# Identity products on TensorE at stage openings and in gaps, and four scale buffers in grouped attention

## What is computed

```python
x = x + tanh(g_xattn[0]) * L0_xattn(layernorm(x), ctx)        # latent attention
x = x + tanh(g_ffn[0])   * L0_ffn(layernorm(x))               # int8 weights
x = x + tanh(g_xattn[1]) * L1_xattn(layernorm(x), ctx)        # plain attention
x = x + tanh(g_ffn[1])   * L1_ffn(layernorm(x))               # memory slots, top 8 of 256
x = x + tanh(g_xattn[2]) * L2_xattn(layernorm(x), ctx, ctx)   # grouped attention, 32 heads of 32
x = x + tanh(g_ffn[2])   * L2_ffn(layernorm(x))               # 4-bit codes, Hadamard turn
x = x + tanh(g_xattn[3]) * L3_xattn(ctx, layernorm(x))        # 16 nearest points, gathered
x = x + tanh(g_ffn[3])   * L3_ffn(layernorm(x))               # top 2 of 8 low-rank experts

def quantize_weight(w):                                       # L2_ffn, both weights
    scale = maximum(max(abs(w), axis=-1) / 7, 1e-8)
    return clip(round(w / scale), -8, 7) * scale
```

## Time and profile before

| what | value |
| --- | --- |
| median of three runs | 2946.02 us (2936.29 to 2954.54) |
| the profiled execution, its own time | 2947.02 us |
| its span in the trace | 2945.2 us |
| mean granted clock of PE | 0.947 |
| PE busy / DVE busy | 90% / 64% |

### The profile page before, as it was taken

One profiled execution on the slowest core, in us unless ns is written; L12 is line 12 of the kernel. 1 busy time (PEld: TensorE's weight loads), 2 busy tenths in 40 slices (PEclk: granted clock), 3 DMA queues, 4 the chain that ended last, 5 costly groups with the idle time before them and its releaser, 6 DMA issues. The chain is left out here.

```text
span 2945.2 us, 50211 instructions
## 1 busy us (share of the span) xinstructions
PE 2654.0 (90%) x18888; PEld 1853.1 (63%) x18892; DVE 1884.9 (64%) x3362; ACT 1070.3 (36%) x2474; POOL 566.4 (19%) x610
## 2 busy tenths in 40 slices
PE   7999999999999489997878899998878999878888
PEld 4665765766656178885645555555557878656664
DVE  5546446456452776666557667677647988966774
ACT  3433433433333333331324444443435555312221
POOL 0110101101101210000024334444412333300000
PEclk9999999999999789998889899998889999988998
DMA  7110101101100655553464456554160001434421
GB/s 263 49 36 14 36 13 49 36 13 49 35 7 1 247 167 151 150 147 121 168 227 139 127 151 172 164 172 143 44 217 16 23 23 45 127 130 172 173 86 38
DMA packets 153764, 304.69 MB, mean 103 GB/s; under 512 B 83936, under 2 KB 107136, under 8 KB 144056
## 3 DMA queue, kind: packets, MB, share of 16 engines
q1 hardware_dynamic: 127064, 229.90, 24.1%
q0 software_dynamic: 19376, 57.15, 6.6%
q10 hardware_dynamic: 7120, 15.01, 1.8%
HBM read 246.39 MB, written 43.04 MB: 98 GB/s over the span
## 5 line engine op out<-in xcount | busy, mean ns | idle before, releaser
L1588 DVE TENSOR_REDUCE latent_nmax<-bank 112x1 f32<-112x487 f32 x128 | 85.2, 666 | 245.8 <-PE bank L1453 238.1
L2260 PE MATMUL bank<-ffn_qT,gather_whole 128*128 128x128 bf16 x3584 | 209.3, 221 | 16.7 <-ACT ffn_us L2383 5.9
L2002 POOL TENSOR_SCALAR grouped_probs<-grouped_probs,grouped_rsum 112x375 f32<-112x375 f32 x256 | 159.6, 642 | 311.8 <-DVE grouped_rsum L2055 311.5
L2260 PEld LDWEIGHTS bank<-ffn_qT,gather_whole 128*128 128x128 fp8e4 x3584 | 205.5, 99 | 21.5 <-issue 20.3
L1376 POOL TENSOR_SCALAR latent_probs<-latent_probs,latent_rsum 112x487 f32<-112x487 f32 x128 | 88.1, 688 | 636.9 <-DVE latent_rsum L1593 636.9
L1949 ACT ACTIVATE grouped_probs<-bank,grouped_nmax 112x375 f32<-112x375 f32 x256 | 143.3, 572 | 117.0 <-DVE grouped_nmax L2051 117.0
L2443 POOL TENSOR_TENSOR ffn_h<-ffn_sl,ffn_us 128x512 f32<-128x512 f32 x56 | 127.8, 2282 | 278.0 <-ACTq L2386 278.0
L1413 PEld LDWEIGHTS bank<-latent_hT,latent_wq 128*128 128x128 f32 x1536 | 175.3, 192 | 7.3 <-issue 7.1
L2051 DVE TENSOR_REDUCE grouped_nmax<-bank 112x1 f32<-112x375 f32 x256 | 122.4, 541 | 83.1 <-PE bank L1860 80.2
L1413 PE MATMUL bank<-latent_hT,latent_wq 128*128 128x112 f32 x1536 | 175.1, 275 | 0.0
L1391 PE MATMUL bank<-latent_wv,latent_hT 128*125 128x384 f32 (+1 forms) x512 | 168.8, 491 | 0.0
(11 more groups left out here) (419 smaller groups left out, 5424.4 us busy)
## 6 DMA issues: line engine op xcount, KB each, us to landing
grouped_raw<-L_weights SPq DMA_DIRECT2D x24, 2048.0 KB, 8.7
points_spread<-numbers SPq DMA_DIRECT2D x16, 912.0 KB
codes<-grouped_flip SPq DMA_DIRECT2D x24, 512.0 KB, 2.6
latent_hT<-ctxT SPq DMA_DIRECT2D x8, 1500.0 KB
plain_ctxT<-ctxT POOLq DMA_DIRECT2D x8, 1500.0 KB
plain_ctx<-ctx POOLq DMA_DIRECT2D x8, 1500.0 KB
grouped_ctx<-ctxT SPq DMA_DIRECT2D x8, 1500.0 KB, 6.6
gather_whole<-numbers SPq DMA_DIRECT2D x12, 912.0 KB
```

Source lines behind the costliest of these rows:

```text
L2002: pool.tensor_scalar(pr[:, g % 2, j, :], pr[:, g % 2, j, :], rsum[:, g % 2, j:j + 1], 1.0, ALU.mult, ALU.mult)\
L2260: mm = pe.matmul(ahead.tile(t)[:, i * P:(i + 1) * P], wgu[:, u0 + f // 4, c:c + 2 * P - 1:2], qT[:, k, :], start=(k == 0), stop=(k == KC - 1))
```

## The change

`kept_busy(pe, C, tile, n)` multiplies the identity by the identity n times into a bank that nobody reads before it is written anew. It stands at the opening of plain_attention (14 times), memory_ffn (16) and hadamard_ffn (22, after a wait for z), before the transposes of memory_ffn's last group (9), before `turned(g, 0)` of the first three quads of grouped_attention (8 each) and before each look of the first 16 rounds of gather_experts (3 each), 133 in all. Where it stands before a wait for data, the wait for the free bank was moved ahead of it. In grouped_attention `scale` gets four slots, `measured(u)` waits for the stores of unit u - 4, and `rounding(u, 0)` waits until unit u - 2 is turned, which frees its slot of `code`. `Norm` packs its three small tiles into one.

```diff
--- before.py
+++ after.py
@@ -265,9 +265,9 @@
 
     def __init__(self, s, n, rows=Q, name="ln"):
         self.stats = s.sb(f"{name}_stats", [rows, n, 2, 6])
-        self.mv = s.sb(f"{name}_mv", [rows, n, 2])
-        roots = s.sb(f"{name}_roots", [rows, 2, n, 1])
-        self.std, self.rstd = roots[:, 0], roots[:, 1]
+        rest = s.sb(f"{name}_mv", [rows, 4 * n])
+        self.mv = rest[:, 0:2 * n].rearrange("p (n c) -> p n c", c=2)
+        self.std, self.rstd = (rest[:, (2 + i) * n:(3 + i) * n].rearrange("p (n c) -> p n c", c=1) for i in range(2))
         self.var_ready = s.sem(f"{name}_var_ready")
         self.std_ready = s.sem(f"{name}_std_ready")
 
@@ -572,6 +572,12 @@
                 pool.tensor_tensor(x[:, b, :], x[:, b, :], bi[:], ALU.add).then_inc(bias_added, 1)
 
 
+def kept_busy(pe, C, tile, n):
+
+    for _ in range(n):
+        pe.matmul(tile[:, 0:P], C.ident[:], C.ident[:], start=True, stop=True)
+
+
 def turn_rows(pe, C, turns, src, name, s, p, n=2, rows=Q):
 
     for h in range(n):
@@ -662,6 +668,7 @@
         @block.tensor
         def _(pe):
             pe.wait_ge(wq_loaded, 16)
+            kept_busy(pe, C, banks.tile[7], 14)
             for s in range(2):
                 pe.wait_ge(z_ready, s + 1)
                 turn_rows(pe, C, first, z[:, s], "zT", s, 0)
@@ -1008,8 +1015,10 @@
             def weights(p):
                 for s in range(size(p)):
                     t = ("wT", p, s)
+                    pe.wait_ge(turns.free(t), turns.count(t, 0))
+                    if p == GROUPS - 1:
+                        kept_busy(pe, C, turns.tile(t), 9)
                     pe.wait_ge(w_ready, p * 2 + (s + 1))
-                    pe.wait_ge(turns.free(t), turns.count(t, 0))
                     for c in range(2):
                         mm = pe.transpose(turns.tile(t)[:, c * P:(c + 1) * P], w[:, s, c * P:(c + 1) * P], C.ident[0:P, 0:P])
                     mm.then_inc(turns.full(t), 1)
@@ -1034,6 +1043,7 @@
                         pe.matmul(turns.tile(t)[0:P, :], vT[:, s * P:(s + 1) * P], wvuT[:, h * 512:(h + 1) * 512], start=True,
                                   stop=True).then_inc(turns.full(t), 1)
 
+            kept_busy(pe, C, banks.tile[7], 16)
             turned(0)
             query(0)
             hidden(0, 0)
@@ -1653,7 +1663,7 @@
         raw, flip = s_.sb("raw", [P, 2, 4 * D]), s_.sb("flip", [P, 16, P], BF16)
         spare_code = spare["wu1T"][:].rearrange("p k n -> p (k n)")
         code, pairs = (spare_code.bitcast(dt).rearrange("p (s n) -> p s n", s=2) for dt in (FP8, BF16))
-        scale, rscale, part = s_.sb("scale", [P, 2, 4]), s_.sb("rscale", [P, 2, 4]), s_.sb("part", [P, 4])
+        scale, rscale, part = s_.sb("scale", [P, 4, 4]), s_.sb("rscale", [P, 2, 4]), s_.sb("part", [P, 4])
         CH = 114
         idx, point, hi, turned_numbers = (raw[:, 0, i * D:(i + 1) * D] for i in range(4))
         idx, turned_numbers = idx.bitcast(U32), turned_numbers.bitcast(BF16)
@@ -1754,7 +1764,7 @@
                 sp.dma_start_transpose(flip[:], pairs[:, u % 2, :]).then_inc(code_turned, 16)
                 sp.wait_ge(code_turned, 16 * (u + 1))
                 sp.dma_start(codes[wall_row(u)], flip[:].rearrange("p t r -> p (t r)").bitcast(U32)).then_inc(code_stored[u % 2], 16)
-                sp.dma_start(scales[wall_row(u)], scale[:, u % 2, :]).then_inc(code_stored[u % 2], 16)
+                sp.dma_start(scales[wall_row(u)], scale[:, u % 4, :]).then_inc(code_stored[u % 2], 16)
 
             def normal(n):
                 if n >= 1:
@@ -1862,9 +1872,11 @@
 
             def turned(g, k):
                 t = ("pT", g, k)
+                pe.wait_ge(turns.free(t), turns.count(t, 0))
                 if k == 0:
+                    if g < 3:
+                        kept_busy(pe, C, turns.tile(t), 8)
                     pe.wait_ge(probs_ready, 4 * g + 4)
-                pe.wait_ge(turns.free(t), turns.count(t, 0))
                 for j in range(4):
                     mm = pe.transpose(turns.tile(t)[0:CT, j * Q:(j + 1) * Q], pr[:, g % 2, j, k * CT:(k + 1) * CT], C.ident[0:Q, 0:Q])
                 mm.then_inc(turns.full(t), 1)
@@ -2012,16 +2024,16 @@
             def measured(u):
                 slot = u % 2
                 dve.wait_ge(raw_loaded[slot], u // 2 * 16 + 16)
-                if u >= 2:
-                    dve.wait_ge(code_stored[slot], u // 2 * 32)
+                if u >= 4:
+                    dve.wait_ge(code_stored[slot], (u // 2 - 1) * 32)
                 for i in range(4):
-                    to = scale[:, slot, i:i + 1] if u % 3 < 2 else part[:, i:i + 1]
+                    to = scale[:, u % 4, i:i + 1] if u % 3 < 2 else part[:, i:i + 1]
                     dve.tensor_reduce(to, raw[:, slot, i * D:(i + 1) * D], AX, ALU.max, apply_absolute_value=True)
                 dve.drain()
 
             def scaled(u):
                 slot, m = u % 2, 4 if u % 3 < 2 else 1
-                sc, rs = scale[:, slot, 0:m], rscale[:, slot, 0:m]
+                sc, rs = scale[:, u % 4, 0:m], rscale[:, slot, 0:m]
                 if m == 1:
                     dve.tensor_reduce(sc, part[:], AX, ALU.max)
                     dve.drain()
@@ -2033,6 +2045,8 @@
 
             def rounding(u, i):
                 dve.wait_ge(raw_scaled, 4 * u + i + 1)
+                if i == 0 and u >= 2:
+                    dve.wait_ge(code_turned, 16 * (u - 1))
                 dve.tensor_scalar(code[:, u % 2, i * D:(i + 1) * D], raw[:, u % 2, i * D:(i + 1) * D], MAGIC, 7.0, ALU.subtract, ALU.min, saturate=False)
                 if i == 3:
                     dve.drain().then_inc(raw_free, 1)
@@ -2261,6 +2275,8 @@
                                                start=(k == 0), stop=(k == KC - 1))
                         mm.then_inc(ahead.full(t), 1)
 
+            pe.wait_ge(z_loaded, 16)
+            kept_busy(pe, C, banks.tile[7], 22)
             entered(0, 0)
             gate_and_up(0, lambda j: pe.wait_ge(gu_loaded[j // 2], 32) if j % 2 == 0 else None)
             pe.wait_ge(wd_loaded, 16 * 3)
@@ -2736,8 +2752,10 @@
                 t = ("look", u)
                 if k == 0 and b > 0:
                     pe.wait_ge(table_ready, b)
+                pe.wait_ge(turns.free(t), turns.count(t, 0))
+                if u < K:
+                    kept_busy(pe, C, turns.tile(t), 3)
                 pe.wait_ge(onehot_ready, u + 1)
-                pe.wait_ge(turns.free(t), turns.count(t, 0))
                 for j in range(KC):
                     for n in range(3):
                         mm = pe.matmul(turns.tile(t)[:, j * RA:(j + 1) * RA], onehot[0:ROWS, u % 3, j * P:(j + 1) * P],
```

## The result

The changed kernel took 2921.78 us (median of 5 runs, 2918.79 to 2928.72) against 2942.27 for the kernel before in the same set (5 runs): a ratio of 0.9939, interval 0.9912 to 0.9965. The medians lie 20.5 us apart; the ratio of the runs says 18. Forecast were 2923 us and 22.9 us saved. By the bound of the prediction this is "within 1%", clear of noise and on the side forecast.

A forecast was written before the change was run, and what follows sets the result against it. PE, busy 90% of the span, was taken as the bound. Terms 21.3 + 2.3 + 0.2 + 1.0 + 1.6 - 3.5 = 22.9 us off 2947.0 gave 2924.1, 2923 us against the median; range 2904 to 2939.

The forecast's parts named there:

- opening 5.9 (6.0 forecast): Grouped attention ahead of batch 0: DVE begins unit 2 earlier, held by its load and no longer by stores; 6.0 us saved.
- 8.2 and 1.7 of clock forecast: Grouped attention, batches 2 to 5: PE's closed gaps save 8.2 us; full clock for batch 2's L1816 records saves 1.7.
- Rival 3: Grouped attention: DVE waits as long for raw to land, so 21.2 us of removed waits go; 2944 us, chance 0.06.
- the rounding's wait: Grouped attention: rounding's new wait for unit u - 2's turning is free, as its stores landed before rounding begins; 0 us.
- memory_ffn, 0.2 + 1.0 forecast: memory_ffn: a clock rise among the opening's products gains 0.2 us; nine hidden products before the last group gain 1.0.
- hadamard_ffn, 1.6 forecast: hadamard_ffn's opening: 22 products raise the clock, end 0.6 us late and gain 2.2 us of turning and L2260; 1.6 net.
- gather, 3.5 lost forecast: gather_experts, first batch: PE sets the pace, 4.3 us lost, 1.0 more at low clock, 1.8 taken up; 3.5 lost.
- The 24 products of grouped attention, 2.1 lost forecast: Products before the first three quads' turning: 0.2 us lost at the first, hidden at the second, 1.9 lost at the third.
- rival 1: Clock stays up through grouped attention's batches 0 and 1, with 1.0 us more in memory_ffn; 2917 us, chance 0.17.
- The clock across transposes: Plain attention's opening: by the skill's page the clock would fall during sixteen transposes, losing 2.3 us; the trace spoke against it.
- rival 2: The clock does not answer to the products: openings' 5.6 us go and 7.1 of delays are paid; 2936 us, chance 0.13.
- rival 4: All that follows shifts against the clock's regulation, causing drops of 1.7 us each; 2950 us with 16 drops, chance 0.04.

The follow-up runs named there:

- run 1: The changed kernel without any of the 133 products, the new waits kept: 2917.35 us, ratio 0.9916 to the kernel before.
- Run 8: The changed kernel, but a unit's first rounding waits for both stores of unit u - 2 instead of its turning: 2924.14 us, ratio 0.9942 to the kernel before.
- run 6: The changed kernel without gather's and grouped attention's products, with memory_ffn's gaps filled (6 before first L1004; 15, 2, 7 in last group): 2912.35 us, ratio 0.9899.
- run 5: The changed kernel without the products of gather, grouped attention and memory_ffn's last group; waits and three openings stay: 2919.96 us, ratio 0.9919.
- run 3: The changed kernel without the three products before each look of gather's first 16 rounds: 2920.13 us, ratio 0.9926 to the kernel before.
- run 9: The changed kernel's waits with products in memory_ffn alone (16 at its opening, then 6, 15, 2 and 7): 2919.49 us, ratio 0.9920 to the kernel before.
- run 2: The changed kernel with all 133 products, but measuring waits for unit u - 2 as before the change: 2948.5 us, ratio 1.0024 to the kernel before.
- run 11: The changed kernel with six products instead of three before each of gather's first 16 looks: 30.68 us from first look to first L2731, 22.53 with three.

## Why the prediction was right, and which terms were not

**The sum held, and in grouped attention by the mechanism named.** That the whole sum came so near is in part luck: memory_ffn, hadamard_ffn and the gather gave 4.8 us less than forecast, grouped and plain attention 3.2 more. Of the 23.4 us that the prediction gave to waits and clock in grouped attention, run 1 shows 23.9 without any product: opening 5.9 (6.0 forecast), 3.3 in batch 0 (from the first L1869 to the second L1883), 3.1 more up to the L1883 behind batch 1's gap (7.0 forecast for the two, 6.4 measured), and 11.6 behind that (8.2 and 1.7 of clock forecast, 9.9). The part mis-sized is the last. 0.7 of it is one more L1816 group that the shorter gap of batch 1 left at a higher clock (3.79 us before, 3.08 in run 1). The four gaps that closed in batches 2 to 5 gave 4.9, 2.7, 2.4 and 1.0 us from one L1883 to the next, 11.0 in all. Of that 1.7 is the clock, as forecast, and 9.3 stand against 8.2: the prediction added up idle times, but a gap of 2.47 us, once closed, brought the next start 2.73 us forward. Measuring started at 1515.07 with the change and at 1515.96 in run 1, against "about 1515.8". Rival 3, waits replaced by equal ones, has fallen (4.5 us of 27.5 came back, the part counted on). Run 8 shows that the rounding's wait is free, and the stronger wait too.

**The products, term by term.** All kernels run the same code in plain attention but for the 14 products: with them nine traces show 316.3 to 322.8 us (mean 320.4), without them four show 322.0 to 323.2 (mean 322.5). That is 2.2 us, against 2.3 forecast, but single traces of one kind lie up to 6.5 us apart. At the opening itself it is more: the first L697 stands 57.0 to 57.6 us behind the first L276 instead of 60.5 to 60.7. Some 3.4 are gained, and over a microsecond of it goes again to later falls of the clock.

- **memory_ffn, 0.2 + 1.0 forecast, 0 measured.** The failed step is the prediction's premise that what is saved at a place moves the end by as much. From the end of plain attention to L950 14.07 us replace 15.35: 1.3 gained (0.2 forecast). From there to the last L1004 the changed kernel takes 86.42 us instead of 84.82, as the stretch at 1.2 GHz after the 1.58 us gap lasted 13.7 us instead of 10.2. The last group gave 0.25 instead of 1.0, as the nine products left the gaps behind them open (run 6).
- **hadamard_ffn, 1.6 forecast, 0 measured.** Eleven of the thirteen traces have 444.9 to 445.4 us for the stage, with products or without (the other two 448.0). The clock's gain at the opening came in six of the nine kernels with the products: L2260's 512 products took 28.7 us. In the other three, the changed kernel among them, the clock fell once more behind the products and they took 30.4. PE's timelines before, in the changed kernel and in run 5:

```profile
2170.91 30.50 PE L2260 MATMUL bank<-ffn_qT,gather_whole 128*128 128x128 bf16 x512 [0.87 <-ACTq L2363]
```

```profile
2145.92 30.37 PE L2274 MATMUL bank<-ffn_qT,gather_whole 128*128 128x128 bf16 x512 [1.13 <-ACTq L2379]
```

```profile
2139.56 28.75 PE L2270 MATMUL bank<-ffn_qT,gather_whole 128*128 128x128 bf16 x512 [1.13 <-ACTq L2375]
```

  Even where it came, the stage was no shorter. Behind it the timeline of PE in run 5 reads

```profile
2168.14 2.00 PE L2284 MATMUL bank<-const_ident,ffn_sd 128*128 128x128 f32 x16
2169.98 1.95 PE L2316 MATMUL bank<-ffn_had,ffn_h 128*128 128x128 f32 x16
2176.72 7.90 PE L2316 MATMUL bank<-ffn_had,ffn_h 128*128 128x128 f32 x48 [4.79 <-ACT ffn_ha L2425]
```

  and that of DVE

```profile
2168.46 1.29 DVE L276 BATCH_NORM_STATS2 ffn_ln_stats<-ffn_z 128x6 f32<-128x512 f32 x2 [4.79 <-DMA ffn_z<-x]
```

  while in the kernel before the same two waits (first PE, then DVE) were

```profile
2207.74 7.34 PE L2304 MATMUL bank<-ffn_had,ffn_h 128*128 128x128 f32 x48 [2.70 <-ACT ffn_ha L2413]
...
2199.48 1.29 DVE L276 BATCH_NORM_STATS2 ffn_ln_stats<-ffn_z 128x6 f32<-128x512 f32 x2 [2.69 <-DMA ffn_z<-x]
```

  DVE waits for the load of the next z, and behind DVE stand ACT and POOL. The load ends 46.5 us after grouped attention has (46.7 in the kernel before), however early PE is, so PE's wait for ACT grows from 2.70 to 4.79 us. SP issues that load behind those of the weights. The failed step: I followed PE's clock and did not look for the next transfer that the stage waits for. This is read from the traces; no run moved the load.
- **gather, 3.5 lost forecast, 5.6 measured** (35.93 against 30.30; 5.4 by run 3). The mechanism was right, PE sets the pace, and a round costs 1.45 us where I took 1.50. The size was off in the two ends: the products ahead of the first look start the chain 0.9 us late, and the batch's last rounds, among them those behind the table, cost another 0.75; the wait for the next table that I took as cover still gave back 0.7 only (1.74 to 1.00) and not 1.8. The cost is less sure than these two traces make it: in runs 5 and 9, which have no such products, the 16 rounds took 33.38 and 33.50 us, with 3.4 us at the low clock among them. Four traces with three products have a mean of 36.0, seven without any 31.4, which makes 4.6 us.
- **The 24 products of grouped attention, 2.1 lost forecast, 0.3 measured** against run 1: some 0.7 gained in batch 0 (some of rival 1) stands against what is lost behind. Over the traces with the new waits, five have a mean of 648.4 us with these products and five of 647.7 without, 0.7 lost.
- **The clock across transposes.** Sixteen transposes lie between the products and L681's first row, and that row and all behind it run at full clock: the 128 records take 24.5 us in all nine traces with the products and 26.8 to 27.0 in the four without. The Trainium skill ("TensorE: Matmul & The Clock Gate", Part 4) says that the transpose mode doesn't count as PE being busy in the same way. The prediction took this to mean that the clock would fall there and the gain be gone; the nine traces show no such fall. In memory_ffn, however, L938's own sixteen records all took the low clock's time (0.24 us each), and in the window of the rise PE was busy for 1.08 of 2.00 us. So the clock rose behind them, and rival 2's "while PE worked without a gap" holds for L681 only.

**Together** the products take away more than they give: 2.2 gained in plain attention, 4.6 to 5.6 lost in the gather, 0.7 lost in grouped attention and nothing elsewhere make 3 to 4 us lost; run 2 measured 7.4 lost (its interval, 1.0009 to 1.0038, is 2.6 to 11 us). So the gain of 20.5 us is some 24 from the waits less what the products cost. The waits alone (2917.35 us) have the lower median, although the interval of 0.9894 to 0.9938 overlaps that of the change. Whether the 3 to 4 us between the two are real stays open.

**The two rows without an edit.** The rest of the gather ran the same code in every kernel, and the thirteen traces show 299.3 to 314.6 us, by where the clock falls (the stage with 314.6 has 65 us at the low clock, that with 299.3 has 38): 311.8 for the kernel before and 302.7 for the changed one are two draws from that, and no effect. The same holds for the 2.2 us ahead of plain attention. The clock does fall at other places from kernel to kernel, as rival 4 has it, but with no sign of its own.

**Which kernel.** Run 6 has the lowest time, 2912.35 us, and the lowest ratio; run 9 shows that the step from the waits alone (2917.35) to it is not settled.

## What to carry to other kernels

A wait for a DMA to have read a slot belongs as late in the program as the slot's reuse allows; here two more slots of a small tile, with the wait moved behind the measuring, freed 24 us, since DVE had stood behind a small store seven times and PE behind DVE. Products that only keep the clock up paid where they filled every gap up to the work meant to be fast (2.1 us, in one group of two kernels), and not where another engine or a load then makes PE wait as long as before; in a loop whose slack is smaller than the products they are plain cost. Judge such edits by the stage in the trace, and only against several traces of unedited stages, since here the spread of one stage (15 us) was larger than all product terms together.

## What was not expected of the hardware

The granted clock fell while PE was busy without a gap. In run 6 the six products closed the gap before L1004, and yet, by PE's timeline,

```profile
1391.71 1.05 PE L1013 MATMUL bank<-mem_wu,mem_hidT 128*128 128x1 f32 x8
1392.62 4.78 PE L981 MATMUL bank<-mem_wvdT,mem_valuesT 128*128 128x64 f32 x32
```

and by its windows (stretch, its us, us that PE was busy and records, granted clock, DMA share, GB/s):

```profile
1392.00:1394.00 2.00, 2.00 (x20) 1.00 1.07 363
1394.00:1396.00 2.00, 2.00 (x17) 0.79 1.10 352
1396.00:1398.00 2.00, 2.00 (x11) 0.50 1.10 349
```

PE is busy for 2.00 of 2.00 us in each, and the clock goes from full to half within the 32 records of L974 (here L981), products whose outputs are 64 columns wide. Run 9 shows the same at 1395 to 1399 (PE busy 4.00 of 4.00 us, mean clock 0.67). So "PE idle" in a trace is not the only thing to look for when the clock falls; what decides was not tried.

A float32 product of 128 columns costs 0.21 to 0.26 us at full clock when it stands in line with others: 39 more in 8.2 us in run 11, and 0.11 to 0.13 us from record to record among the products of the changed kernel. The prediction had 0.23.
